# Audio tower on one core: segments of 25 outputs in the first two layers, results sorted into even and odd planes by the transpose, and a new order of slots

## The reference

```
CONVS = [(128, 10, 5)] + [(128, 3, 2)] * 4 + [(128, 2, 2)] * 2
for w, g, b, s in zip(conv_ws, ln_gs, ln_bs, strides):
    h = _conv1d(h, w, s)
    h = _fp32_layernorm(h, g, b)          # over the channels
    h = jax.nn.gelu(h, approximate=False)
norm_h = _fp32_layernorm(h, fln_g, fln_b)
out = norm_h @ proj_w + proj_b
h = h + attention(layernorm(h))
h = h + experts(layernorm(h))             # route 0 and the chosen one of 9
```

## Time and profile before

| | us |
|---|---|
| three timed runs | 581.24, 583.17, 583.61 (median 583.17) |
| the profiled execution | 581.46 |
| its span, first to last instruction | 579.7 |
| PE busy | 549.2 of the span |
| DVE, ACT, POOL busy | 318.1, 316.5, 264.4 |

### The profile page before, as it was taken

One profiled execution on the slowest core, in us unless ns is written; L12 is line 12 of the kernel. 1 busy time (PEld: TensorE's weight loads), 2 busy tenths in 40 slices (PEclk: granted clock), 3 DMA queues, 4 the chain that ended last, 5 costly groups with the idle time before them and its releaser, 6 DMA issues.

```text
span 579.7 us, 11208 instructions
## 1 busy us (share of the span) xinstructions
PE 549.2 (95%) x4191; PEld 517.1 (89%) x4191; DVE 318.1 (55%) x751; ACT 316.5 (55%) x499; POOL 264.4 (46%) x297
## 2 busy tenths in 40 slices
PE   6899999999999999999999999999999996899995
PEld 5697999989999999999999989989898975789995
DVE  4666465565567666856574666554654443612231
ACT  1566666747665675558455846574554423344440
POOL 4674394693248426732754294324423030133443
PEclk9999999999999999999999999999999996799999
DMA  6191000792000000000000000000000069051110
GB/s 178 42 329 41 1 1 11 182 211 43 2 1 11 2 6 1 1 7 1 2 0 7 1 1 2 6 1 1 6 2 5 3 174 223 19 158 38 49 38 11
DMA packets 17519, 26.35 MB, mean 45 GB/s; under 512 B 2172, under 2 KB 13397, under 8 KB 17467
## 3 DMA queue, kind: packets, MB, share of 16 engines
q1 hardware_dynamic: 14155, 15.85, 10.1%
q0 software_dynamic: 3296, 9.78, 7.2%
q10 hardware_dynamic: 16, 0.00, 0.0%
HBM read 17.13 MB, written 9.18 MB: 45 GB/s over the span
## 4 chain that ended last, share of the span: by engine, by line
PE 82%; POOL 7%; DVE 4%; ACT 4%; issue 2%; DMA 1%; SPq 1%; POOLq 0%; DVEq 0%; ACTq 0%
PE ps L759 23%; PE ps L751 9%; PE ps L771 7%; PE ps L748 7%; POOL rstd L597 5%; PE ps L1015 4%; PE ps L824 4%; PE ps L1004 3%; PE ps L1003 3%; PE ps L845 3%; PE ps L815 2%; PE ps L886 2%; PE ps L749 2%; PE ps L753 2%; PE ps L906 2%
## 5 line engine op out<-in xcount | busy, mean ns | idle before, releaser
L603 POOL TENSOR_TENSOR rstd<-ssum,neghalf 128x4 f32<-128x4 f32 (+7 forms) x128 | 116.9, 914 | 194.3 <-DVE ssum L1089 194.1
L759 PE MATMUL ps<-wt,wide 128*128 128x128 f32 (+2 forms) x1248 | 151.0, 275 | 4.6 <-ACT wide L1397 4.6
L1378 ACT ACTIVATE work<-ps 128x512 f32<-128x512 f32 (+7 forms) x128 | 67.2, 525 | 161.3 <-PE ps L753 81.9
L759 PEld LDWEIGHTS ps<-wt,wide 128*128 128x128 f32 (+2 forms) x1248 | 144.2, 184 | 7.5 <-issue 6.2
L1089 DVE TENSOR_REDUCE ssum<-work 128x4 f32<-128x516 f32 (+7 forms) x128 | 76.0, 594 | 69.7 <-ACT work L1378 69.2
L1098 DVE TENSOR_TENSOR work<-ps,rstd 128x512 f32<-128x512 f32 (+7 forms) x128 | 76.2, 595 | 68.5 <-POOL rstd L603 67.8
L1397 ACT ACTIVATE wide<-ps,lncol 128x512 f32<-128x512 f32 (+6 forms) x120 | 109.5, 912 | 5.7 <-PE ps L771 5.3
L597 POOL TENSOR_TENSOR rstd<-var,half 128x10 f32<-128x10 f32 (+2 forms) x39 | 82.9, 2133 | 9.0 <-DVE var L1056 8.4
L1408 ACT ACTIVATE h<-ps,lncol 128x512 f32<-128x512 f32 (+1 forms) x120 | 82.0, 730 | 2.4 <-PE ps L824 2.4
L751 PE MATMUL ps<-wt,h 128*128 128x256 f32 x304 | 74.9, 380 | 0.0
L771 PE MATMUL ps<-ident,work 128*128 128x128 f32 (+2 forms) x424 | 66.2, 270 | 0.5 <-DVE work L1098 0.2
(11 more groups left out here) (227 smaller groups left out, 833.6 us busy)
## 6 DMA issues: line engine op xcount, KB each, us to landing
sorted_tokens<-zero POOLq DMA_DIRECT2D x1, 5886.5 KB, 33.9
W2s<-in_L_ffn_W_dram SPq DMA_DIRECT2D x9, 576.0 KB, 8.7
wide<-in_L_ffn_W_dram SPq DMA_DIRECT2D x8, 576.0 KB
cols<-sorted_tokens SPq DMA_DIRECT2D x13, 96.5 KB, 2.0
xnat<-in_x_dram SPq DMA_DIRECT2D x7, 135.0 KB
wt<-in_L_ffn_b_dram SPq DMA_DIRECT2D x1, 864.0 KB, 4.4
wide<-in_L_tok_conv_w_dram SPq DMA_DIRECT2D x4, 192.0 KB, 3.4
common_sums<-acc POOLq DMA_DIRECT2D x1, 579.0 KB, 5.3
```

Of the source, the lines that this page charges most:

```text
L603: gp.tensor_tensor(rstd[0:rows, idx, 0:count], ssum[0:rows, idx, 0:count], neghalf[0:rows, 0:count], ALU.pow).then_inc(rstd_done, 1)
L759: last = nc.tensor.matmul(y[0:rows, j * C:(j + 1) * C], h[l - 1][g % 2][:, at:at + rows], wt[:, TAP0[l] + tap, :], start=(tap == 0), stop= ...
L1378: nc.scalar.activation(sq[0:rows, n % 2, 0:CUTS[l][k], 0:C], ybank(n)[0:rows, 0:w].rearrange("p (j c) -> p j c", c=C), ACT.Square).then_in ...
```

## The change

1. `LEN1` is 25 instead of 26, so layer 1 has 25 blocks per group (chunks of 4, 4, 4, 4, 4, 4, 1), `LOCALS` is 51, and the rows of a block in layers 2 to 5 fall from 128, 120, 104, 104 to 124, 116, 100, 100.
2. With an odd segment length, the parity of an output's position depends on the segment too. The `turn` of layer 1 now writes each transposed block split by the parity of the segment: neighbouring columns go alternately to two places 128 or 384 elements apart. `gelu` of layer 1 becomes two instructions per chunk, one for each plane, of at most 256 columns each and with a step of 25 elements.
3. The last run of token steps (group 7): the attention mask is put into PSUM by two matmuls ahead of `qkv`, and the scores are added to it there; DVE no longer adds the mask, takes the maximum from PSUM and subtracts in the same way; half of `copy_probs` moves to ACT; a one-element Exp stands ahead of the real one.
4. All runs: `choose` compares the logits with their maximum directly, and `lgb` is written after `hot`.
5. The jobs of `AFTER` use banks 4, 5, 0 and 1 in turn; the buffers `xcol` alternate across groups.
6. `BODY`, `HEAD`, `LAST`, `DRAIN` and the tables `RUN_n` are re-ordered.
7. Buffers' lengths, padding and `h[5]`'s layout follow.

The core of the diff (the other rows of the tables and the lines on padding are left out):

```diff
-LEN1 = 26
-ROWS_OF = [P, P, P, 120, 104, 104, 104]
-LOCALS = 2 * LEN1 + 2
+LEN1 = 25
+ROWS_OF = [P, P, 124, 116, 100, 100, 104]
+LOCALS = 2 * LEN1 + 1
...
-CUTS = [None, (4, 4, 4, 4, 4, 4, 2), (4, 3, 3, 3), (4, 3), (4,), (2,), (1,)]
+CUTS = [None, (4, 4, 4, 4, 4, 4, 1), (4, 3, 3, 3), (4, 3), (4,), (2,), (1,)]
...
-    ((2, -1, 3), [('z', 1, 0), ('z', 1, 1)], [('pow', 1, 0), ('pow', 1, 1)]),
-    ((1, 0, 2), [('xt', 0, 4)], [('pow', 1, 2)]),
-    ((6, -2, 0), [('l0', 0, 4, 0), ('l0', 0, 4, 1)], [('pow', 1, 3)]),
-    ((1, 0, 4), [('l0', 0, 4, 2)], [('pow', 1, 4), ('xs', 1, 0)]),
...
+    ((1, 0, 2), [('z', 1, 0)], [('pow', 1, 1)]),
+    ((2, -1, 3), [('z', 1, 1), ('xt', 0, 4)], [('pow', 1, 0)]),
+    ((6, -2, 0), [], []),
+    ((1, 0, 4), [('l0', 0, 4, 1), ('l0', 0, 4, 0)], [('xs', 1, 0)]),
...
+BANK = [4 + n % 4 if n < HEAD_JOBS else 4 + n % 2 if n < len(JOBS) - len(AFTER) else 4 + n % 2 if n % 4 < 2 else n % 2
+        for n in range(len(JOBS))]
...
-                    last = nc.tensor.transpose(tr[:, j * rows:(j + 1) * rows],
-                                               xh[0:rows, n % 2, j * C:(j + 1) * C], ident[0:rows, 0:rows])
+                    to = tr[:, j * rows:(j + 1) * rows]
+                    if l == 1:
+                        i, d = divmod(j, 2)
+                        at = tr[:, d * P + i * 64:d * P + i * 64 + 1]
+                        to = bass.AP(at.tensor, at.offset, [at.ap[0], [1, P // 2], [P if d else 3 * P, 2]])
+                    last = nc.tensor.transpose(to, xh[0:rows, n % 2, j * C:(j + 1) * C], ident[0:rows, 0:rows])
                 last.then_inc(tr_done, 1)
...
+                    if r == NT - 1:
+                        for half in range(2):
+                            nc.tensor.matmul(ps[0:M, half, 0:3 * M], ident[0:M, 0:M], mask[:, :].unsqueeze(1).to_broadcast([M, 3, M]),
+                                             start=True, stop=False)
...
-                        last = nc.tensor.matmul((pa, pb)[half][0:M, 0:3 * M], qs[:, half, :],
-                                                kpad[:, half, :, :].rearrange("p h k -> p (h k)"), start=True, stop=True)
+                        o = (pa, pb)[half] if r < NT - 1 else ps[:, half, :]
+                        last = nc.tensor.matmul(o[0:M, 0:3 * M], qs[:, half, :], kpad[:, half, :, :].rearrange("p h k -> p (h k)"),
+                                                start=(r < NT - 1), stop=True)
                     last.then_inc(t["sc"], 1)
...
+                    if r == NT - 1:
+                        pe.wait_ge(s_half, 1)
...
+                if step == "mask" and r == NT - 1:
+                    ve.wait_ge(t["sc"], r + 1)
+                    nc.vector.reduce_max(mx[:, :], masked, axis=X).then_inc(t["mx"], 1)
+                if step == "mask" and r < NT - 1:
...
                 if step == "less_max":
                     ve.wait_ge(t["mx"], r + 1)
-                    nc.vector.tensor_tensor(t1[:, :, :], t1[:, :, :], mx[:, :].unsqueeze(2).to_broadcast([M, NH, M]),
-                                            ALU.subtract).then_inc(t["sub"], 1)
+                    if r < NT - 1:
+                        nc.vector.tensor_tensor(t1[:, :, :], t1[:, :, :], mx[:, :].unsqueeze(2).to_broadcast([M, NH, M]),
+                                                ALU.subtract).then_inc(t["sub"], 1)
+                    else:
+                        nc.vector.tensor_tensor(t1[:, :, :].rearrange("p (a h) k -> p a h k", a=2), masked,
+                                                mx[:, :].rearrange("p (a h) -> p a h", a=2).unsqueeze(3).to_broadcast([M, 2, 3, M]),
+                                                ALU.subtract).then_inc(t["sub"], 1)
...
-                    for half in range(2):
+                    for half in range(2 if r < NT - 1 else 1):
                         last = nc.vector.tensor_copy(pT[:, 3 * half:3 * half + 3, :],
                                                      (pa, pb)[half][0:M, 0:3 * M].rearrange("p (h k) -> p h k", h=3))
...
-                    nc.vector.tensor_scalar(lgb[:, r, :], pb[0:M, 0:NE], best[:, 0:1], None, ALU.subtract).then_inc(t["less"], 1)
-                    ve.wait_ge(t["less"], r + 1)
-                    nc.vector.scalar_tensor_tensor(out=cand[:, :], in0=lgb[:, r, :], scalar=0.0, in1=iota[:, :],
+                    nc.vector.scalar_tensor_tensor(out=cand[:, :], in0=pb[0:M, 0:NE], scalar=best[:, 0:1], in1=iota[:, :],
                                                    op0=ALU.is_lt, op1=ALU.add).then_inc(t["cand"], 1)
                     ve.wait_ge(t["cand"], r + 1)
                     nc.vector.tensor_reduce(best[:, 1:2], cand[:, :], axis=X, op=ALU.min).then_inc(t["best"], 1)
                     ve.wait_ge(t["best"], r + 1)
                     nc.vector.tensor_scalar(hot[:, r, :], iota[:, :], best[:, 1:2], None, ALU.is_equal).then_inc(t["hot"], 1)
+                    nc.vector.tensor_scalar(lgb[:, r, :], pb[0:M, 0:NE], best[:, 0:1], None, ALU.subtract).then_inc(t["less"], 1)
...
+                if l == 1:
+                    w = (count + 1) // 2
+                    for d in range(2):
+                        v = slice(0, 2) if count > 1 else slice(d, d + 1)
+                        src = tr[:, :].rearrange("p (v d i m) -> p d v i m", v=2, d=2, m=P // 2)[:, d, v, 0:w, :]
+                        shift = (LEN1 + 1 - d) // 2
+                        at = h[1][g % 2][:, d * EVEN[1] + lo // 2 + shift * v.start:d * EVEN[1] + lo // 2 + shift * v.start + 1]
+                        to = bass.AP(at.tensor, at.offset, [at.ap[0], [shift, v.stop - v.start], [1, w], [LEN1, P // 2]])
+                        last = nc.scalar.activation(to, src, ACT.Gelu, bias=lncol[:, 9:10], scale=lncol[:, 1:2])
+                    last.then_inc(act_done, 1)
+                    return
...
                 if step == "exp":
+                    if r == NT - 1:
+                        nc.scalar.activation(r0[:, 1:2], eps[0:1, :], ACT.Exp)
                     ac.wait_ge(t["sub"], r + 1)
                     nc.scalar.activation(t1[:, :, :], t1[:, :, :], ACT.Exp, scale=SCALE).then_inc(t["ex"], 1)
+                if step == "copy_probs" and r == NT - 1:
+                    ac.wait_ge(t["pT"], r + 1)
+                    ac.wait_ge(t["den"], r + 1)
+                    nc.scalar.copy(pT[:, 3:6, :], pb[0:M, 0:3 * M].rearrange("p (h k) -> p h k", h=3)).then_inc(s_half, 1)
...
-            ac.wait_ge(t["cand"], NT)
+            ac.wait_ge(t["less"], NT)
```

91 lines of the change are left out of this document (47 added, 44 removed), and 55 rows, old and new, of tables (BODY, HEAD, LAST).

## The result

The changed kernel takes **565.06 us** (median of 4 runs, 564.36 to 568.76), the kernel before 583.39, timed beside it (4 runs, 581.24 to 585.61). The ratio is 0.970, with a 95% interval of 0.964 to 0.976: faster by 3.0%. The forecast was 570, so the sign was right and about 5 us more were gained than predicted. The profiled execution took 564.38 us (span 562.6), 17.1 less than that of before, against 12.9 forecast.

What follows compares the result with a forecast made beforehand. PE was taken to bound the body. Savings of 9.3, 2.2 and 1.35 us, with two terms at 0, summed to -12.9, taking the profiled 581.46 to 568.6 and the median to 570; range 563 to 579.

Steps and rivals of the forecast that it cites:

- term 1: PE's removed work in convs, transposes, l0 and z: 1.16 us a group, times 8 groups, -9.3 us.
- term 2: Layer-6 convolution's wait for layer 5's GELU: 0.43 us saved in each of the body's five groups, -2.2 us.
- Reading of the bound: Body: PE is the bound, with a matmul under way 53.64 of 54.5 us a group; not in the last run.
- Comes off the time nearly one for one: Body: work PE no longer does shortens the time almost equally; added ACT work is free unless PE waits.
- Counted as nothing: Convs of layers 2 to 5: loading 4 fewer rows of stationary data was taken to save nothing.
- rival B: The new order makes waits of its own: 4 to 8 us back, 574 to 578, up to 580; chance 0.15.
- Term 3: Last token run: mask matmuls, DVE additions, Exp table, turn_probs to values, choose and six up jobs, sum -1.35 us.
- Term 4: Layer 1's GELU in two instructions: ACT works 0.15 us longer per chunk, hidden by two PE slots, 0 on the path.
- Term 5: Layer 1's transposes with split outputs: stepped PSUM writes taken as 0; bounds 0 or +22 us.
- A: Stepped writes slow layer 1's transposes: 592 us at double length, range 583 to 605; chance 0.10.
- C: Last run: the clock doesn't fall or comes back sooner: 565 us, range 560 to 566; chance 0.09.
- D: No change: what PE no longer does is turned into waiting; chance 0.04.

Runs made afterwards that it cites:

- e1: Changed kernel with the order tables (slots, job places, token places) of the kernel before, keeping the new sizes and code: 576.64 us (ratio 0.989).
- e2: Kernel before with the changed kernel's order tables and transposed-window buffers chosen by running number, segments still 26 long: 573.88 us (0.985).
- e5: Changed kernel with 12 of layer 2's 13 blocks loading 128 stationary positions instead of 124: 565.63 us (0.969).
- e11: Kernel before with 24 matmuls nobody reads filling five idle stretches of PE in its last token run: 579.26 us (0.994).
- e7: Changed kernel with 19 matmuls nobody reads ahead of five waits of PE in the last token run: 560.48 us (0.962).
- e4: Changed kernel with the job up(2, 5) two slots earlier, ahead of scores in the last token run: 564.87 us (0.971).
- e6: Changed kernel plus 15 unread bf16 matmuls ahead of the last run's turn_probs, five writing adjacent places, ten in steps: 563.71 us, one run.
- e3: Changed kernel with the last run's mask, copy, one-element Exp and bank changes undone, keeping the shorter choose and all tables: 566.28 us (0.973).
- e10: Changed kernel with last-run fillers, up(2, 5) ahead of scores, and three unread matmuls behind each of the head's first two xt: 559.62 us (0.960).
- e8: Changed kernel with unread matmuls ahead of five last-run waits, ten before turn_probs, and up(2, 5) ahead of scores: 560.59 us (0.963).

## Why the prediction was right, and where it was off

- **The time.** The forecast was 570, measured are 565.06, inside the range of 563 to 579. The sum of 12.9 us against 17.1 by the two traces hides errors that partly cancel: term 1 too large by 2.8, term 2 too small by 4.9, the input that arrives 1.5 earlier not seen at all, and the last stretch too small by 0.6. That the total is off by no more is in part luck.
- **Reading of the bound: right.** PE bounds the body. "Comes off the time nearly one for one" is true only together with the new order: with the old one (e1) the group's period falls by 0.51 us for 1 us less work. One reading of the rows was wrong: the eight waits of the earlier trace rows are those of a line that serves layers 2 to 6, and only six of them, 3.9 us, are of a layer-6 convolution. The sum used one of them, 0.63, five times, and is not touched.
- **Term 1, PE's work, -9.3: right in the body, too large outside it.** Per group 53.50 (e2) becomes 52.46: -1.04, forecast -1.16. But the eightfold of it isn't reached. From e2 to the changed kernel the stretches ahead of (6,7,0) give 8.0, and 1.5 of these are the input; 6.5 remain for 9.3. The removed block is part of the reason: in the head and in LAST a `turn` now waits 0.53 and 0.47 us for ACT behind the one-block chunk, and e1, with the old order, has these waits too (0.52 and 0.97), so they come with the new sizes. "Counted as nothing" was wrong by some 0.1 us a group for layer 2 (e5), hidden in that sum by other parts that gave less.
- **The input's load, 0: missed.** A shorter segment is also a shorter row to load, and PE starts on it 1.5 us earlier. The prediction has no term for it.
- **Term 2, the order, -2.2: the most mis-sized term.** The order by itself gives 9.0 us (e2), and 11.6 between e1 and the changed kernel; ahead of (6,7,0) it is 7.1 by the traces. Three things were missed. Half of `z` was priced at 0.44 us, its matmul of 240 columns and 0.03 for that of 30; the two take 0.58 (0.43 and 0.15), so the wait of the layer-6 convolution fell by 0.60 from start to start and not by 0.43. The wait of `turn_1`, 0.23 of the 0.86 idle of the earlier trace rows, was taken as staying; it is gone, and since it is gone wholly it was worth 0.40. And the sum stopped at the body's five groups: 0.9 and 1.6 us of e2's gain lie ahead of (6,0,0) and behind (6,4,0). What made me keep the saving small was rival B's thought that the new order makes its own waits; in the body none is seen.
- **Term 3, the last run, -1.35: right.** The pair at an equal clock, e11 and e7, gives 1.5. The parts, from the traces of before and after: `scores` starts 0.39 later behind (6,7,0) (forecast +0.5, for the mask matmuls); `scores` to Exp 3.64 before and 3.30 now, -0.34 (forecast -0.85 + 0.6 = -0.25); `turn_probs` to `values` 2.52 and 1.84, -0.68 (-0.6); the six `up` -0.58 (-0.75); `logits` to `rank` 1.68 and 1.47, -0.21 (-0.25). Together -1.42. That the table load behind `up` holds Exp up is shown by e4.
- **Term 4, GELU in pairs, 0: right in the body**, +0.13 on ACT and no wait there; its argument, that two slots of PE hide it, fails where the one-block chunk follows, as said under term 1. How much of these two waits is the pair and how much the shorter `conv` wasn't separated. **Term 5, stepped writes, 0: right**, and for the reason given: a stepped stream delivers a column each 0.84 ns (e6), and a transpose needs 0.85.
- **Rivals.** A was refuted, by next to no margin (0.85 against 0.84 ns a column). B came only as the two waits outside the body, and by the sizes, not by the order. C didn't come, and e7 gives its price: 3.7 us of the span, near the 5 that I gave it. D is what e1 shows in half.
- **Chance.** Nine traces have the new sizes, the new order and `z` in halves. They start (6,0,0) at 116.3 to 116.7, or, where the granted clock falls in the head (0.80 to 0.82 from 20 to 26 us in e3, e5 and e6), at 118.1 to 118.4. The profiles of before and after both have the clock at 1.00 there, so the 17.1 us are free of this; the medians, 18.3 apart, need not be.

## What to carry to other kernels

Where one engine is busy all the time, a shorter program and the order that fits it are one change: tried apart, the work gave 6.3 us and the order 9.0, together 18.3. Price what you move into a wait by the starts of its own rows (`z` was 0.58, not 0.44), and a wait that goes away wholly from start to start of the instructions around it, not by the idle time shown; add up all waits of the period, not the largest. What holds in the body need not hold at the ends of the program: look there for a place where the removed work was what covered a wait, and for loads that got shorter too. An idle stretch of PE can cost more behind it than in it: look for a low granted clock after each one, and fill it if nothing useful can stand there.

## What was not expected of the hardware

- A matmul that writes PSUM in steps delivers a column each 0.84 ns, adjacent writes one each 0.43 ns (e6: bf16, 256 columns, the 2.4 GHz level, one run). Steps of 2 words and of 128 words cost alike.
- 124 stationary columns in place of 128 save some 3 ns in each row of an fp32 matmul at 128 streamed columns (0.112 to 0.109 us, e5); 116, 104 and 100 save no more than 124.
- The same program falls to the 1.2 GHz level in some executions and not in others, in the head after two idle stretches of 0.83 us: 0.82 granted from 20 to 26 us in e3, 1.00 in the profile of the changed kernel. With these stretches filled to 0.16 us (e10), five runs lay within 0.21 us; without that, e8's four lay within 2.4 and the changed kernel's four within 4.4.
